# Two decoder layers on one core: the third normalisation of layer 1 is moved beside the cross-attention heads, and GpSimd takes over three small jobs

## The reference

```python
x = _layernorm(x + _L0_attn_ref(...));  x = _layernorm(x + _L0_xattn_ref(...));  x = _layernorm(x + _L0_ffn_ref(...))
x = _layernorm(x + _L1_attn_ref(...))    # 16 heads of 16, causal
x = _layernorm(x + _L1_xattn_ref(...))   # keys and values of all 8 sequences together, 1024 of them
x = _layernorm(x + _L1_ffn_ref(...))     # 256 -> 768 -> 256, fp8 weights, per-channel scales
```

## Time and profile before

| | us |
|---|---|
| median of three executions | 1445.62 |
| the profiled execution's own time | 1444.57 |
| its span in the trace | 1442.8 |
| PE busy | 1288.0 (89%) |
| DVE busy | 1072.3 (74%) |
| ACT busy | 685.8 (48%) |
| POOL busy | 102.2 (7%) |

### The profile page before, as it was taken

The page is one execution under the profiler, slowest core; times in us unless marked ns, Lnnn a source line. Parts: engine busy times, 40 slices in busy tenths (PEclk is TensorE's granted clock), DMA queues, the critical chain, the costliest instruction groups (busy, mean ns, idle before and its releaser), DMA issues.

```text
span 1442.8 us, 24457 instructions
## 1 busy us (share of the span) xinstructions
PE 1288.0 (89%) x9108; PEld 854.2 (59%) x9113; DVE 1072.3 (74%) x2477; ACT 685.8 (48%) x1286; POOL 102.2 (7%) x95
## 2 busy tenths in 40 slices
PE   6979999998999999999999999988898589898676
PEld 3647667666766766766766676656777322222334
DVE  6778578678578677757767755746888899999467
ACT  2336335435534633633543453523444388888232
POOL 2210010020010011001002000000000000000001
PEclk9989999999999999999999999999999655555689
DMA  7321002001100100100200032002000199999000
GB/s 242 149 98 61 12 12 65 12 4 35 39 12 16 62 12 15 62 12 11 65 12 1 19 102 69 20 23 95 9 8 5 30 177 183 176 182 173 18 1 30
DMA packets 174789, 83.96 MB, mean 58 GB/s; under 512 B 137936, under 2 KB 170064, under 8 KB 174416
## 3 DMA queue, kind: packets, MB, share of 16 engines
q1 hardware_dynamic: 173520, 82.03, 23.6%
q10 hardware_dynamic: 1152, 0.36, 0.1%
HBM read 43.57 MB, written 5.24 MB: 34 GB/s over the span
## 4 chain that ended last, share of the span: by engine, by line
PE 59%; DVE 26%; ACT 5%; issue 5%; DMA 3%; POOL 1%; SPq 0%; DVEq 0%; POOLq 0%; ACTq 0%
PE ps_t L1807 12%; PE ps_p L1791 11%; PE ps_s L2040 7%; DVE w_moe L1682 7%; PE ps_o L1957 5%; PE ps_o L1947 4%; PE ps_o L1872 4%; PE ps_o L2040 3%; PE ps_p L1849 3%; DMA w_moe<-w_moe 3%; DVE probs L1203 2%; PE ps_s L1849 2%; PE ps_o L1876 2%; DVE row_max L1209 1%; DVE w_moe L1684 1%
## 5 line engine op out<-in xcount | busy, mean ns | idle before, releaser
L1807 PE MATMUL ps_t<-ident,probs 128*128 128x128 f32 x1072 | 170.4, 280 | 28.6 <-ACT probs L1022 8.0
L882 ACT ACTIVATE probs<-probs 128x512 f32<-128x512 f32 x184 | 115.6, 628 | 136.8 <-DVE probs L1203 136.8
L1807 PEld LDWEIGHTS ps_t<-ident,probs 128*128 128x128 f32 x1072 | 123.3, 142 | 78.1 <-issue 37.9
L844 ACT ACTIVATE probsT<-ps_t 128x512 f32<-128x512 f32 x232 | 136.5, 589 | 64.0 <-PE ps_t L1807 63.7
L2040 PE MATMUL ps_s<-w_moe,xbT 128*128 128x352 f32 x352 | 121.9, 471 | 0.0
L1791 PE MATMUL ps_p<-w_qkv,xinT 128*128 128x512 f32 (+1 forms) x240 | 105.1, 562 | 11.3 <-DMA xinT<-in_xT 7.4
L2274 PEld LDWEIGHTS ps_p<-vals,w_moe 128*128 128x128 f16 x1024 | 37.4, 106 | 120.1 <-DMA w_moe<-w_moe 100.6
L797 POOL TENSOR_TENSOR rms<-mean_sq,neg_half 128x8 f32<-128x8 f32 x40 | 67.1, 1679 | 269.2 <-DVE mean_sq L1237 269.2
L844 ACT ACTIVATE bigT<-ps_t 128x512 f32<-128x512 f32 (+1 forms) x128 | 69.0, 553 | 33.3 <-PE ps_t L1807 31.3
L2040 PEld LDWEIGHTS ps_s<-w_moe,xbT 128*128 128x128 f32 x352 | 64.1, 194 | 22.0 <-issue 1.4
L1872 PE MATMUL ps_o<-v_all,probsT 128*128 128x128 f32 x512 | 70.6, 282 | 6.6 <-DVE big L1267 6.2
(11 more groups left out here) (317 smaller groups left out, 2679.9 us busy)
## 6 DMA issues: line engine op xcount, KB each, us to landing
w_out<-in_wT_out SPq DMA_DIRECT2D x8, 2048.0 KB, 8.5
w_moe<-in_wT_gu SPq DMA_DIRECT2D x1, 5632.0 KB, 17.6
w_moe<-in_wT_down SPq DMA_DIRECT2D x1, 2816.0 KB, 10.1
keys<-keys2T SPq DMA_DIRECT2D x8, 256.0 KB, 2.0
keys2T<-keys SPq DMA_DIRECT2D x1, 2048.0 KB, 10.2
w_moe<-w_moe SPq DMA_TRANSPOSE x128, 3.3
w_qkv<-in_wT_qkv SPq DMA_DIRECT2D x3, 512.0 KB, 4.9
w_qkv<-in_wT_qkv SPq DMA_DIRECT2D x1, 1536.0 KB, 8.2
```

The source lines that it names most:

```text
L844: nc.scalar.activation(dst, src.bitcast(BF16) if dst.dtype == BF16 else src, ACT.Copy)\
L882: nc.scalar.activation(probs[:, at % 4, :], probs[:, at % 4, :], ACT.Exp).then_inc(L0.exped, 1)
L1807: ins = nc.tensor.transpose(dst[:, i * P:(i + 1) * P], src(i), ident_b[:] if bf else ident[:])
```

## The change

Four things change.

1. **Four tiles beside the shared heads.** `out_turn`, `out_project`, `in5`, `out5`, `x5_turn` and the three-part split of tiles 0 to 3 are placed at fixed heads of the tiles that follow: for a finished tile t-1, PE transposes at head 9, ACT copies at head 9, PE projects at head 12, DVE adds and takes the statistics at head 13 and norms at head 14; the split of tile t-2 lies at heads 0, 1, 3, 4 and 6. The results stand in the tile's own bank of `ps_p` (`tile_bank`), so PE waits for `rest5` before it reuses that bank.
2. **GpSimd takes the bias** of every head's exponential (L1684 before). DVE signals the maximum through the new semaphore `maxed2`, POOL computes and signals `max2_ready`.
3. **GpSimd takes, after the heads,** the last bf16 part of tiles 4 to 7 and of all 12 blocks (`x5_last`, `fuse_last`), and the normed tiles of `out5` (4 to 7) and `out6` (all).
4. **The third pass is overlapped one block deep**: ACT runs `gate(b + 1)`, `fuse_first(b)`, `fuse_second(b - 1)`, DVE runs `gate_up_block(b)`, `fuse_rest(b - 1)`, `in6(b - 9)`, POOL runs `fuse_last(b - 2)`, `out6(b - 9)`. Block 0 is issued on PE between the last sums of the heads; all four last tiles collect outside `ps_p`, in `ps_t` and in the banks of block 10.

```diff
+            for u in range(TILES * H1):
+                t, h = u // H1, u % H1
+                q2s, max2 = q2ss[:, t], lane_of(t).max2
+                pool.wait_ge(maxed2, u + 1)
+                nc.gpsimd.tensor_scalar(max2[:, 1, h:h + 1], max2[:, 0, h:h + 1], q2s[:, 2, h:h + 1], LN255, ALU.mult,
+                                        ALU.add).then_inc(max2_ready, 1)
+                if 1 <= t <= HT and h == IN5:
+                    power1(N5, t - 1)
+            def norm_out(N, t, dst):
+                power1(N, t)
+                pool.wait_ge(N.rstd_ready, t + 1)
+                nc.gpsimd.tensor_scalar(dst, N.res[t % LANES], N.mean_var[t % LANES][:, 0:1], N.rstd[t % LANES],
+                                        ALU.subtract, ALU.mult).then_inc(N.x_ready, 1)
+            def fuse_last(b):
+                pool.wait_ge(fsecond, b + 1)
+                nc.gpsimd.tensor_tensor(fusep[b][:, 2, :], tmpf[:, b % 2, :], fusep[b][:, 1, :], ALU.subtract)\
+                    .then_inc(fparts, 1)
...
@@ ScalarE, in the loop over the heads
+                if 1 <= t <= HT and h == OQ_TAKE:
+                    oq_take(t - 1)
+                if 2 <= t <= HT + 1 and h == X5_FIRST:
+                    x5_first(t - 2)
+                if 2 <= t <= HT + 1 and h == X5_SECOND:
+                    x5_second(t - 2)
...
@@ VectorE, in the loop over the heads
-                    link1(nc.vector.tensor_reduce(max2[:, 0, h:h + 1], flat(shared_scores(u)[:]), X,
-                                                  ALU.max))
-                    nc.vector.tensor_scalar(max2[:, 1, h:h + 1], max2[:, 0, h:h + 1], q2s[:, 2, h:h + 1], LN255,
-                                            ALU.mult, ALU.add).then_inc(max2_ready, 1)
+                nc.vector.tensor_reduce(max2[:, 0, h:h + 1], flat(shared_scores(u)[:]), X, ALU.max).then_inc(maxed2, 1)
+                if t >= 1 and h == TURN_LAG:
+                    take_shared(t - 1)
+                if 1 <= t <= HT and h == IN5:
+                    in5(t - 1)
+                if 1 <= t <= HT and h == OUT5:
+                    out5(t - 1)
+                if 2 <= t <= HT + 1 and h == X5_REST:
+                    x5_rest(t - 2)
+                if 2 <= t <= HT + 1 and h == X5_LAST:
+                    x5_last(t - 2)
...
+            for b in range(IB, 2 * IB):
+                d = b - IB - 3
                 gate_up_block(b)
+                fuse_rest(b - 1)
                 if d >= 0:
                     in6(d)
...
@@ TensorE, after the scores and sums of unit u
+                if 1 <= t <= HT and h == OQ_TURN:
+                    out_turn(t - 1)
+                if 1 <= t <= HT and h == OUT2:
+                    out_project(t - 1)
+                if 2 <= t <= HT + 1 and h == X5_TURN:
+                    x5_turn(t - 2)
+                if u == HEADS:
+                    pe.wait_ge(exp2, HEADS - 2)
+                    out_turn(HT)
+                    out_turn(HT + 1)
+                if u == HEADS + 1:
+                    out_project(HT)
+                if u == HEADS + 2:
+                    out_turn(HT + 2)
+                    gate_and_up(0)
+                if u == HEADS + 3:
+                    out_project(HT + 1)
...
+            x5_turn(HT)
+            out_project(HT + 2)
+            gate_and_up(1)
+            x5_turn(HT + 1)
+            out_turn(LAST)
+            gate_and_up(2)
+            out_project(LAST)
+            x5_turn(HT + 2)
+            gate_and_up(3)
+            gate_and_up(4)
+            x5_turn(LAST)
+            gate_and_up(5)
+            gate_and_up(IB)
+            gate_and_up(IB + 1)
+            for b in range(IB + 2, 2 * IB):
                 gate_and_up(b)
+                down(b - IB - 2)
+            last_blocks(HT, range(IB - 1))
+            last_blocks(HT + 1, range(IB - 1))
+            pe.wait_ge(fused, 2 * IB - 1)
+            last_blocks(HT + 2, range(IB - 1))
+            last_blocks(LAST, range(IB - 1))
+            for d in range(HT, TILES):
+                last_blocks(d, [IB - 1]).then_inc(last_down, 1)
```

More of the change, by code:

```diff
@@ L234, in projections1 @@
     keys += [("av", t) for t in range(TILES)]
-    keys += [("out2", t) for t in range(TILES)] + [("down", t) for t in range(HT + 2)]
+    keys += [("down", t) for t in range(HT)]
     return [(key, n) for key, n in keys if n is not None]
@@ L579, in decoder @@
         heads_2 = sem("heads_2")
+        oq_turned = sem("oq_turned")
+        oq_taken = sem("oq_taken")
+        out2_done = sem("out2_done")
+        x5_turned = sem("x5_turned")
+        second5 = sem("second5")
         parts5 = sem("parts5")
@@ L1085, in _ @@
             act.wait_ge(scaled_scales, 1)
[L1086 to L1098, removed]
+            oq_take(HT)
+            oq_take(HT + 1)
+            gate(0)
+            oq_take(HT + 2)
+            x5_first(HT)
+            gate(1)
+            fuse_first(0)
+            x5_first(HT + 1)
+            x5_second(HT)
+            oq_take(LAST)
+            gate(2)
+            fuse_first(1)
+            fuse_second(0)
+            x5_second(HT + 1)
+            gate(3)
+            fuse_first(2)
+            fuse_second(1)
+            x5_first(HT + 2)
+            gate(4)
+            fuse_first(3)
+            fuse_second(2)
+            x5_second(HT + 2)
+            fuse_first(4)
+            x5_first(LAST)
+            gate(5)
+            fuse_second(3)
+            x5_second(LAST)
+            fuse_first(5)
+            fuse_second(4)
+            gate(6)
+            for b in range(IB, 2 * IB):
+                if b + 1 < 2 * IB:
+                    gate(b + 1)
+                fuse_first(b)
+                fuse_second(b - 1)
+            fuse_second(2 * IB - 1)
         @block.vector
@@ L1750, in _ @@
-            x5_last(HT - 1)
-            for b in range(2 * IB):
-                n, x = beside(b)
-                d = b - IB - 2
+            in5(HT)
+            in5(HT + 1)
+            gate_up_block(0)
+            take_shared(LAST)
+            x5_rest(HT)
+            gate_up_block(1)
+            in5(HT + 2)
+            fuse_rest(0)
+            x5_rest(HT + 1)
+            gate_up_block(2)
+            in5(LAST)
+            fuse_rest(1)
+            gate_up_block(3)
+            x5_rest(HT + 2)
@@ L1754, in _ @@
+            fuse_rest(2)
+            gate_up_block(4)
+            x5_rest(LAST)
+            fuse_rest(3)
+            gate_up_block(5)
+            fuse_rest(4)
+            for b in range(IB, 2 * IB):
+                d = b - IB - 3
                 gate_up_block(b)
-                if n is not None:
-                    in5(n)
+                fuse_rest(b - 1)
                 if d >= 0:
                     in6(d)
-                fuse_rest(b)
-                if n is not None:
-                    out5(n)
@@ L1762, in _ @@
[L1762 to L1775 removed]
+            fuse_rest(2 * IB - 1)
+            for d in range(HT - 1, TILES):
+                in6(d)
         @block.tensor
```

251 lines of the change are left out of this document (119 added, 132 removed).

## The result

The changed kernel takes 1431.35 us (median of five, 1429.87 to 1434.53). The kernel before took 1445.62 us beside it (median of five, 1440.58 to 1446.64), so the ratio is 0.9914 [0.9896, 0.9933]: 0.9% faster. The forecast was 1431.5. The profiled execution is the slowest of the five (1434.53, span 1432.4).

A forecast was written before the change was run, and what follows sets the result against it. DVE was taken to set the pace in the heads, PE and ACT less than 15% behind, and a chain of waits to rule most of the rest. Heads +15, rest -29, sum -14 us: 1431.5 us, range 1415 to 1450.

The forecast's parts named there:

- every sign that I named for a wrong forecast: Heads growing by less than 8 or more than 25 us, or the rest taking more than 88.
- The ring: Heads: three bank pairs share a round trip including POOL's bias; distance between units 1.42 us, 5.5 us more in all.
- x: Heads: the time of POOL's bias within the round trip of 3.83 + x, taken as 0.45 us.
- The pieces: Heads: ten pieces of work per tile, 7.4 us, of which 4.0 remain; 16 us for four tiles.
- The late transposes: Heads: transposing DMAs come late less often when units are farther apart, -3.5 us.
- two engines that close: First half of the blocks: PE's 24 us and DVE's 23 do not hide each other fully; 5 us added, 29 in all.
- The end: From the end of block 11: DVE's chain of four statistics keeps its 21.1 us.
- The collisions: Behind the heads: long POOL instructions run against DVE instructions with two SBUF inputs; 3 us added.
- rival 2: Last pass: POOL and DVE block each other, the gain shrinks to 20 us, time 1440.5; chance 0.14.
- Rival 1: Heads: the three bank pairs become the bound through the bias; at 1.2 us for it 1455; chance 0.14.
- rival 3: Heads: the pieces are hidden, the heads grow by only 3 us, time 1419.5; chance 0.17.
- rival 4: Blocks: late tile parts, PE stands 5 to 8 us before block 6, first half 35; time 1440.5; chance 0.08.

The follow-up runs named there:

- e3: The kernel before with only the bias of the exponential moved to POOL: 1444.76 us, ratio 0.9996 to the kernel before.
- e7: The changed kernel with the last bf16 part of all 12 blocks back on DVE: 1429.36 us.
- e8: The changed kernel with the eight last normed tiles back on DVE, their powers staying on POOL: 1430.77 us.
- e2: The changed kernel with POOL computing every bias twice, the first time into a spare column: 1438.96 us.
- e1: The changed kernel with the bias of the exponential back on DVE, all else as changed: 1435.46 us.
- e6: The changed kernel with tile 7's split moved ahead in the orders of ACT, DVE and POOL: 1429.11 us.
- e5: The changed kernel with POOL writing the last parts of blocks 10 and 11 before the waiting normed tiles: 1427.18 us.
- f1: The changed kernel with four filler matmuls, never read, before the value products of each unit on PE: 1494.38 us.
- e4: The changed kernel with PE issuing the projection of tiles 0 to 3 twice, same result: 1434.98 us.

## Why the prediction was right, and which terms weren't

The total is right: -14 forecast, -14.3 in the medians, -12.9 in the stretches. The mechanism is right too: heads up and rest down by more, every sign that I named for a wrong forecast absent (heads up by 11.9, rest 83.1). That the number fits this well is luck. The terms beneath are less good, and the errors offset each other: the heads cost 3 us less than forecast, the rest gave back 4 less.

Where the gain comes from, the experiments show by elimination: with the bias alone on POOL there is none (e3), and without POOL's twelve subtractions (e7) or its last normed tiles (e8) it stays. What is left is that block 0 starts 2.9 us after the last exponential instead of 24.3, and the overlap of the blocks. No run separates these two.

**The ring.** Right as a mechanism, shown by e2. x is 0.27 us (120 of 128 biases at 0.26 to 0.27), not 0.45; the formula 3.83 + x gives 4.10 against 4.04 measured (the signal from POOL to ACT takes 0.04 us in most units, not 0.11), and the free distance is 1.35 instead of 1.42. That is less than the 1.38 before, so the term of +5.5 us has the wrong sign: it is about -4. The value I gave for x = 0.21 (1.35, 4 us less) is what came. Two of three free distances are 1.28, which is PE's own, and the third is 1.48: PE stands just behind the ring. In order of time, at tile 1's projection:

```profile
1187.32 1.22 DVE L1811 TENSOR_REDUCE w_moe<-ps_s 128x1 f32<-128x1024 f32 x1
1188.60 1.23 DVE L1811 TENSOR_REDUCE w_moe<-ps_o 128x1 f32<-128x1024 f32 x1
1188.64 0.27 POOL L840 TENSOR_SCALAR w_moe<-w_moe 128x1 f32<-128x1 f32 x1 [1.01 <-DVE w_moe L1811]
1188.73 2.05 PE L2355 MATMUL ps_p<-w_qkv,attT 128*128 128x256 f32 x4
1190.72 1.03 PE L2396 MATMUL ps_t<-keys2T,w_moe 48*128 48x512 bf16 x2
1191.79 1.22 DVE L1811 TENSOR_REDUCE w_moe<-ps_t 128x1 f32<-128x1024 f32 x1 [1.96 <-PE ps_t L2396]
...
1192.93 0.41 DVE L1671 TENSOR_TENSOR xa<-ps_p,w_moe 128x256 f32<-128x256 f32 x1
...
1194.52 0.15 DVE L1681 TENSOR_SCALAR w_moe<-w_moe 128x1 f32<-128x1 f32 x1
1194.59 1.22 DVE L1811 TENSOR_REDUCE w_moe<-ps_s 128x1 f32<-128x1024 f32 x1
```

**The pieces.** From maximum to maximum these are 3.19 us over the projection and 2.80 over the statistics: 1.84 and 1.45 above the free distance. I had 1.6 and 1.35. The small pieces vanish almost whole, as I said (0.4 us over heads 0 to 6 of a tile). Tiles 1 to 4 take 26.5, 26.7, 26.4 and 26.3 us, against 23.7, 23.4, 24.1 and 23.5 before. These 11 us have the bias's gain in them. The pieces alone are the step from e3 to the changed kernel, 188.5 to 202.1: 13.5 us where I had 16. With the bias on DVE (before to e1) they cost 15.9.

**The late transposes.** This step failed. I wrote that they come late less often when units are farther apart (-3.5). That much the traces bear out: PE waits 8.0 us for them in e1 and in e2, where units are farther apart, and 11.6 in the changed kernel. But the changed kernel's distances are not longer than before, they are shorter. Tiles 0, 5, 6 and 7, which have no pieces or only the small ones of the split, take 23.5, 23.1, 24.2 and 22.5 us against 23.1, 23.2, 23.6 and 22.9 before, though 16 free distances are 21.6 and were 22.1. In e3, where the bias alone moved, about 4 us of such hiccups came in addition instead of 3.5 going away. The waits for a maximum in the changed heads, us in total, times, longest:

```profile
ACT w_moe L1139 <- POOL w_moe L840: 36.0, 42, 2.8
DVE w_moe L1811 <- PE ps_t L2396: 13.6, 18, 2.2
```

DVE has its idle time in few long waits for PE (13.6 us in 18 for this pair, 24.9 in 39 for all three), not in a small one at every unit. Together: for the bias alone I had 5.5 (ring) - 3 (takes) - 3.5 (transposes) = -1, and e3 shows about -4, -1.5 and +4, in all -1.7; each of the three was off and the sum came right by luck. The pieces then add 13.5 instead of 16, which makes 11.9 and not 15.

**Behind the heads.** To block 0 it took 2.9 instead of 1.6. The first half is 25.9 where I had 29: my 5 for "two engines that close" was too much. A gap of PE of 1.95 lies in it, where I had said under 1: the transposes of a tile wait for its normed tile on POOL. The wait before block 6 was 3.44, plus 1.65 lost to the clock in one of two profiles, where I had 2.1; e6 shows that the order of tile 7's split was the cause of the part of the wait above 1.4.

**The end** is the term that was wrong: I kept 21.1 us from the end of block 11 and measured 27.9. I had counted what the normed tile costs POOL (a little over DVE's 0.41, where it is 1.23 to 1.37), but not whom it stands in front of: block 10's last part. e5 shows 5.0 of the 6.8 us to be this order; the other 1.8 stay open.

**The collisions** (3 allowed) exist, smaller than rival 2. After, in order of time:

```profile
1366.31 1.23 POOL L848 TENSOR_SCALAR w_moe<-xa,w_moe 128x256 f32<-128x256 f32 x1
1367.50 1.16 POOL L866 TENSOR_TENSOR keys2T<-probs,keys2T 128x512 bf16<-128x512 f32 x1
1367.86 1.08 DVE L1677 TENSOR_TENSOR kdup<-kdup,w_qkv 128x256 f32<-128x256 f32 x1
```

DVE's addition takes 0.42 alone and 1.08 here: it ends 0.28 after POOL's subtraction. Over all that runs behind the heads, DVE's instructions take 4.7 us more than the shortest of their line and shape; before it was 0.5, and without POOL's subtractions (e7) it is 0.7. Not all of it lies on the path. The Trainium skill, SBUF — State Buffer, Who interferes with whom, speaks of an exclusive lock between the two, and the trace agrees. The subtraction is 1.16 (taken 1.3). e7 shows that with all 12 of them gone the time falls by 2 us, most of it at the end, where the queue is.

Rival 1 fell with x = 0.27, rival 3 with the 2.8 us by which each of four tiles is longer, rival 4 with the first half at 25.9; its wait before block 6 was real (3.44), but not its price of 9.

## What to carry to other kernels

When work moves to an idle engine, follow its whole queue: an instruction that waits for late data holds up the ready ones behind it, and here this cost 5 us beside a gain of 14. In a ring of three buffers, an instruction moved off the busiest engine still costs a third of its length plus signals per unit if it stays in the round trip; compare the two numbers (4.04 / 3 against 1.38) before counting the engine's relief. And look at what waits second in the loop: here a shorter distance between units came with longer waits for transposing DMAs, and most of what it gave was gone.

## What the runs showed of the hardware that I had not expected

- POOL's subtraction, scaling by two per-partition scalars (one input, 128x256, fp32), takes longer than its two-input subtraction of the same number of columns (which writes bf16 and not fp32). POOL's groups by form behind the heads of the changed kernel (busy us, mean ns, idle before):

```profile
L866 POOL TENSOR_TENSOR keys2T<-probs,keys2T 128x512 bf16<-128x512 f32 x5 | 6.2, 1246 | 2.0 <-ACT keys2T L1162 2.0
L848 POOL TENSOR_SCALAR xc<-bigT,w_moe 128x256 f32<-128x256 f32 x4 | 5.2, 1302 | 0.4
L861 POOL TENSOR_TENSOR w_out<-bigT,w_out 128x256 bf16<-128x256 f32 x4 | 2.9, 717 | 5.3 <-ACT w_out L1130 5.3
```

  1302 ns against 717. The Trainium skill, GPSIMD Engine Reference, Engine selection, calls one-input operations on GpSimd "roughly line-rate" beside VectorE; here DVE takes 0.41 us for the same tile, and the trace disagrees.
- On one column POOL's `tensor_scalar` takes 0.27 us, half of its one-column power (0.56), and little more than DVE's 0.21.
- The granted clock stayed at its lower level while PE was busy 50.00 of 50 us (f1), and rose for 3.4 us behind a doubled fp32 projection in a stretch with gaps (e4).
- DVE's one-input normed tile is held up by POOL's subtraction as its two-input instructions are: 1.16 instead of 0.41 (e8). Why it is isn't shown.
